# Linear attention: new order of steps (second scores ahead of values), whole tiles for the text block, copied text columns

## What is computed

```python
q = phi(x @ W_Q.T); k = phi(x @ W_K.T); v = x @ W_V.T      # phi(u) = elu(u) + 1
S = g4 * S + einsum('bhi,bhj->bhij', kt, vt)                # for each token t
z = g3 * z + kt
num = einsum('bhij,bhi->bhj', S, qt)
den = sum(z * qt, axis=-1, keepdims=True) + EPS
y = (num / den) * sigmoid(x @ W_g_w.T + W_g_b)
h = h + y @ W_O.T
h = h + quantised_ffn(layernorm(h))                         # Hadamard, 4 bits, ternary weights
```

## Time and profile before

| | us |
|---|---|
| median of 3 runs (654.33, 652.72, 647.9) | 652.72 |
| span of the profiled execution | 652.8 |
| TensorE busy, matmuls | 572.1 |
| VectorE busy | 412.4 |
| ScalarE busy | 280.9 |
| GpSimd busy | 219.3 |
| from scores(1, 1), 157.7, to scores(7, 1), 363.6 | 205.9 |

### The profile page before, as it was taken

How to read it: one execution, slowest core, us unless ns; L and a number is a source line. 1 busy time by engine, 2 the same in 40 slices (tenths; PEclk the granted TensorE clock), 3 DMA queues, 4 the chain that set the end, 5 groups by cost and what they waited for, 6 DMA issues and landing times. The chain is left out here.

```text
span 652.8 us, 11678 instructions
## 1 busy us (share of the span) xinstructions
PE 572.1 (88%) x4050; PEld 477.6 (73%) x4050; DVE 412.4 (63%) x1037; ACT 280.9 (43%) x590; POOL 219.3 (34%) x323
## 2 busy tenths in 40 slices
PE   5899859899999999899999977678887999999883
PEld 4799738677787879687868665356676899998772
DVE  2598966667778777788777775766476332222156
ACT  1533334343636455473827223474611355555310
POOL 2467760401011111111102010675003577777500
PEclk9999958899999999999999976769999999999988
DMA  7222103000000000000000060421100233333277
GB/s 231 73 62 68 40 27 97 2 1 2 1 1 2 3 0 2 2 1 1 2 2 1 3 240 2 103 68 49 49 2 24 73 101 103 106 104 101 88 226 209
DMA packets 27445, 37.03 MB, mean 57 GB/s; under 512 B 4542, under 2 KB 22783, under 8 KB 27391
## 3 DMA queue, kind: packets, MB, share of 16 engines
q1 hardware_dynamic: 23166, 24.78, 12.6%
q0 software_dynamic: 4224, 11.54, 5.7%
HBM read 25.95 MB, written 10.35 MB: 56 GB/s over the span
## 5 line engine op out<-in xcount | busy, mean ns | idle before, releaser
L1629 POOL TENSOR_TENSOR c_rstd<-c_ve,mhalf 128x2 f32<-128x2 f32 (+2 forms) x20 | 13.4, 671 | 158.3 <-DVE c_ve L564 158.3
L665 PE MATMUL ps<-b_x_hi,wa_hi 128*128 128x288 f32 x192 | 58.8, 306 | 6.0 <-DVE w1raw L1385 4.4
L2714 DVE TENSOR_TENSOR w1raw<-ps,w1raw 128x192 f32<-128x192 f32 x43 | 15.4, 358 | 68.2 <-ACT w1raw L2494 68.2
L666 PE MATMUL ps<-b_x_lo,wa_hi 128*128 128x288 f32 x192 | 57.3, 298 | 0.0
L667 PE MATMUL ps<-b_x_hi,wa_lo 128*128 128x288 f32 x192 | 57.2, 298 | 0.0
L2783 POOL DMA_INDIRECT kv<-x_rows,r_src_i x43 | 41.8, 971 | 27.1 <-issue 10.7
L1678 POOL TENSOR_TENSOR w1raw<-w1raw 128x288 f32<-128x288 f32 x16 | 16.1, 1027 | 97.8 <-DVE w1raw L1385 97.8
L1240 ACT CAST b_y_hi<-b_yt 128x256 fp32r<-128x256 f32 x32 | 12.9, 402 | 81.3 <-DVE b_yt L1367 81.2
L2307 PE MATMUL ps<-w,w1raw 96*128 x172 | 44.5, 381 | 1.3 <-ACT w1raw L2506 1.3
L665 PEld LDWEIGHTS ps<-b_x_hi,wa_hi 128*128 128x128 f32 x192 | 36.7, 191 | 9.0 <-DVE w1raw L1385 6.0
L1379 DVE TENSOR_TENSOR w1raw<-ps,decay 128x960 f32<-128x960 f32 x32 | 36.5, 1155 | 8.3 <-PE ps L1025 8.3
(11 more groups left out here) (389 smaller groups left out, 1640.5 us busy)
## 6 DMA issues: line engine op xcount, KB each, us to landing
d_x<-y_rows SPq DMA_DIRECT2D x18, 256.0 KB, 4.3
w1raw<-in_W_t SPq DMA_DIRECT2D x8, 384.0 KB, 6.0
x_rows<-w1raw SPq DMA_DIRECT2D x6, 384.0 KB, 2.5
a_xt<-in_x_t SPq DMA_DIRECT2D x8, 256.0 KB, 3.6
a_xfl<-in_x_flat SPq DMA_DIRECT2D x8, 256.0 KB, 2.8
out<-hres SPq DMA_DIRECT2D x16, 128.0 KB, 3.9
w<-in_W_t SPq DMA_DIRECT2D x8, 192.0 KB, 4.7
w1raw<-in_Ws_t SPq DMA_DIRECT2D x1, 768.0 KB, 8.7
```

Of the source, the lines that this page charges most:

```text
L665: nc.tensor.matmul(out, x_hi, w_hi, start=start, stop=False)
L666: nc.tensor.matmul(out, x_hi, w_lo, start=False, stop=False)
```

## The change

Five things, in one diff of which this is the core:

- Text block on whole tiles. Scores multiply 128 keys, so that the text keys stand in the rows where the text tile has them (`text_keys` begins 32 (b mod 4) columns ahead of the text columns of `held`; key tiles now lie ahead of query tiles there), and values use all 128 rows. The mask is zero outside the batch's own 32 rows: `move_strip` (GpSimd) writes this strip of `g["decay"]` for each batch, and `mask(b, 0)` waits for it.
- Text columns copied. Only batches 0 and 4 transpose text rows; in the others `copy_text` (GpSimd) copies 32 columns of `x_hi` and `x_lo` from the starting batch's text tile, two batches ahead.
- Other waits in `projections`: exp_done in place of phi_done, and the text values in bank 6, behind pair 2.
- Other orders: scores 2 ahead of values 0, values 2 ahead of turn_unit (TensorE); unit_sums and mask 2 ahead of take 0, quantise ahead of phi 1 (VectorE); unit_norm ahead of round_y 0 (ScalarE).
- The normalisation of rows is done a step earlier (b + 3 in place of b + 2), at the step's end.

```diff
-    return T + P if starts(b) else T
+    return T + P if starts(b) else L
+def text_copies(b):
+    return b - b // NQ
...
     for fc in range(FC):
         bank = rows_bank(b) + fc
         for t in range(2):
-            nc.tensor.transpose(ps[:, bank, t * P:(t + 1) * P], xn[:, t, fc * P:(fc + 1) * P], ident[:])
+            mm = nc.tensor.transpose(ps[:, bank, t * P:(t + 1) * P], xn[:, t, fc * P:(fc + 1) * P], ident[:])
         if starts(b):
             nc.tensor.transpose(ps[:, bank, T:T + P], xn_text[:, fc * P:(fc + 1) * P], ident[:])
-        mm = nc.tensor.transpose(ps[:, bank, L:T], xn_text[q, fc * P:(fc + 1) * P], ident[q, q])
+            mm = nc.tensor.transpose(ps[:, bank, L:T], xn_text[q, fc * P:(fc + 1) * P], ident[q, q])
...
-            first = (NP, NP + 2, 0, 2)[i]
+            first = (0, 2, NP, NP + 2)[i]
             return slice(first, first + 2)
+        def text_keys(b, j):
+            return slice(j * T + L - TXT * (b % NQ), j * T + L - TXT * (b % NQ) + P)
...
-                        mm = split_products(nc, ps[:, (6, 7, 4)[t], :], x_hi[:, b % 2, fc, rows],
+                        mm = split_products(nc, ps[:, (6, 7, 6)[t], :], x_hi[:, b % 2, fc, rows],
...
             def projections(b):
                 pe.wait_ge(lo_done, b + 1)
+                if not starts(b):
+                    pe.wait_ge(text_copied, text_copies(b))
...
-                pe.wait_ge(phi_done, NP * b + 1)
+                pe.wait_ge(exp_done, NP * b + 1)
+                pair(b, 2)
                 if starts(b):
+                    pe.wait_ge(v_read, v_count(b) + 1)
                     value_rows(b, (2,))
-                    pe.wait_ge(v_read, v_count(b + 1))
-                pair(b, 2)
-                pe.wait_ge(phi_done, NP * b + 2)
+                pe.wait_ge(exp_done, NP * b + 2)
                 pair(b, 3)
                 if b >= 2:
                     turn_q(b - 2)
-                pe.wait_ge(v_read, v_count(b) + 1)
+                pe.wait_ge(v_read, v_count(b + 1))
                 pair(b, 4)
-                pe.wait_ge(phi_done, NP * b + 3)
+                pe.wait_ge(exp_done, NP * b + 3)
...
-                    m, n = ROWS[s], WIDTHS[s]
-                    keys = slice(0, P) if s < 2 else text_rows(b)
+                    n = WIDTHS[s]
+                    keys = slice(j * T + s * P, j * T + s * P + P) if s < 2 else text_keys(b, j)
                     for r in range(2):
                         rows = slice(DK * r, DK * r + DK)
-                        mm = nc.tensor.matmul(ps[keys, bank(j) + r, col:col + n],
-                                              qk[rows, NP + j, s * P:s * P + m],
-                                              qk[rows, j, T - n:T], start=True, stop=True)
+                        mm = nc.tensor.matmul(ps[:, bank(j) + r, col:col + n], held[rows, keys],
+                                              qk[rows, NP + j, T - n:T], start=True, stop=True)
...
-                    keys = slice(0, P) if s < 2 else text_rows(b)
+                    rows = v[:, s] if s < 2 else v_text
                     for r in range(2):
                         h = 2 * j + r
                         mm = nc.tensor.matmul(ps[DK * r:DK * r + DK, 6 + j % 2, T - n:T],
-                                              v[:, s, h * DK:(h + 1) * DK] if s < 2 else
-                                              v_text[keys, h * DK:(h + 1) * DK], a[keys, j % 2, r, col:col + n],
+                                              rows[:, h * DK:(h + 1) * DK], a[:, j % 2, r, col:col + n],
...
                 if is_batch(b):
                     scores(b, 1)
+                    scores(b, 2)
                     values(b, 0)
                     values(b, 1)
-                    scores(b, 2)
                     scores(b, 3)
+                    values(b, 2)
                 if is_unit(u):
                     turn_unit(u)
                 if is_batch(b):
-                    values(b, 2)
                     values(b, 3)
...
             def round_x(b):
                 ge(act, gate_done, 2 * (b - 1))
+                if starts(b):
+                    act.wait_ge(text_copied, text_copies(b - 1))
...
-                if is_batch(b):
-                    round_y(b, 0)
                 if is_unit(u):
                     unit_norm(u)
                 if is_batch(b):
+                    round_y(b, 0)
                     round_y(b, 1)
-                if 2 <= b + 2 < B:
-                    rows_norm(nc, g, act, b + 2)
...
                     exps(n, 1)
+                    exps(n, 2)
                     if starts(n):
                         copy_v_text(n)
-                    exps(n, 2)
                     exps(n, 3)
...
+                if 2 <= b + 3 < B:
+                    rows_norm(nc, g, act, b + 3)
...
-            nc.vector.memset(ps[:, 0:2, T:], 0.0)
-            for q in range(1, NQ):
-                last = nc.vector.tensor_copy(g["decay"][TXT * q:TXT * q + TXT, :, AW - TXT:AW],
-                                             g["decay"][0:TXT, :, AW - TXT:AW])
+            step(nc.vector.memset(strips[:], 0.0))
+            for q in range(NQ):
+                nc.vector.memset(strips[text_rows(q), q:q + 1], 1.0)
+                last = nc.vector.tensor_copy(text_decay[text_rows(q), :, :], g["decay"][0:TXT, :, AW - TXT:AW])
...
             def mask(b, j):
+                if j == 0:
+                    ge(dve, strip_set, b)
...
                 if is_batch(b):
                     mask(b, 1)
-                    take(b, 0)
                 if is_unit(u):
                     unit_sums(u)
                 if is_batch(b):
+                    mask(b, 2)
+                    take(b, 0)
                     take(b, 1)
-                if 2 <= b + 2 < B:
-                    rows_sums(nc, g, dve, b + 2)
-                if is_batch(b):
-                    mask(b, 2)
                     mask(b, 3)
                     take(b, 2)
...
+                if is_unit(u):
+                    quantise(u)
                 if is_batch(n):
                     phi(n, 1)
                 if b == -1:
                     ffn_weights()
-                if is_unit(u):
-                    quantise(u)
...
+                if 2 <= b + 3 < B:
+                    rows_sums(nc, g, dve, b + 3)
                 if is_batch(n):
                     invert(n)
                     mask(n, 0)
...
+            def move_strip(b):
+                pool.wait_ge(pick_set, 4)
+                pool.wait_ge(masked, NP * b)
+                nc.gpsimd.tensor_scalar(g["decay"][:, :, AW - TXT:AW], text_decay[:],
+                                        strips[:, b % NQ:b % NQ + 1], None, ALU.mult).then_inc(strip_set, 1)
+            def copy_text(b):
+                first = T + TXT * (b % NQ)
+                pool.wait_ge(lo_done, b - b % NQ + 1)
+                ge(pool, gate_done, 2 * (b - 1))
+                nc.gpsimd.tensor_copy(x_hi[:, b % 2, :, L:T], x_hi[:, 0, :, first:first + TXT].bitcast(F32))
+                nc.gpsimd.tensor_copy(x_lo[:, b % 2, :, L:T], x_lo[:, 0, :, first:first + TXT].bitcast(F32)
+                                      ).then_inc(text_copied, 1)
...
-                if 2 <= b + 2 < B:
-                    rows_root(nc, g, pool, b + 2)
+                if 1 <= b + 2 < B and not starts(b + 2):
+                    copy_text(b + 2)
                 if is_unit(u - 1):
                     agent_root(u - 1)
+                if is_batch(b) and is_batch(n):
+                    move_strip(n)
                 if is_batch(n):
                     pool.wait_ge(phi_done, NP * n + 3)
                     for j in range(NP // 2):
                         pool.wait_ge(z_done, NP * n + j + 1)
-                        nc.gpsimd.tensor_tensor(z[:, j, :], z[:, j, :], qk[:, j, 0:T], ALU.mult).then_inc(qz_done, 1)
+                        nc.gpsimd.tensor_tensor(z[:, j, :], z[:, j, :], qk[:, NP + j, 0:T], ALU.mult
+                                                ).then_inc(qz_done, 1)
+                if 2 <= b + 3 < B:
+                    rows_root(nc, g, pool, b + 3)
```

## The result

The changed kernel takes 632.81 us in the median of 4 runs (626.41 to 634.6), the kernel before 653.33 us beside it (647.9 to 654.33): a ratio of 0.969, 95% interval 0.964 to 0.975. By these ratios the change is worth 20 and 23 us; 23.0 us were predicted. Ratios are taken over the fast runs of both kernels, medians over all runs. The profiled execution has a span of 624.7 us and is the shortest of its four, so its 28.1 us less than the profiled span before overstate the gain, and part of what follows is about which 5 to 8 us of it are not the change's.

The account below looks back on a forecast made before the run. VectorE's queue was taken to end each front, and TensorE's rear to stand at waits for phi and c_qi. The terms, the largest -11.1 us for the front, summed to -23.0 us from 652.8: 629.8 us, range 620 to 644 us.

Parts of the forecast that it names:

- Part 1: Rear, pairs 2, 3 and 5: waiting on exp_done, not phi_done, removes six stalls of 0.77 us, -4.6 us.
- part 2: Projections of a starting batch: text values in bank 6 behind pair 2 remove one wait, 0.84 us of it real, -0.8 us.
- A: Rival, text groups: whole tiles cost more than the drains they save, about 0.7 us a step, 636 us; chance 0.10.
- B: Rival: ScalarE and GpSimd are late instead, front gains only 0.6 us a step, gates hold output, 640 us; chance 0.16.
- E: Rival, front: the new order gains nothing because values 2 waits for take 0; 12.0 us go, 642 us; chance 0.09.
- D: Rival: TensorE's waits at values 2 and rotate bring the lower clock, one stretch a step, 24 us, 654 us; chance 0.05.
- C: Rival: batch 0 keeps full clock, GpSimd doesn't slow VectorE, the tail behind batch 7 shortens, 625 us; chance 0.08.
- Part 6: Scores and values: whole text tiles remove gaps and small loads, mostly hidden in fronts; exposed in scores 0, -0.5 us.
- part 5: Front, batches 1 to 7: VectorE's new queue puts rotate 8.7 us after scores 1, -11.1 us; turn_unit's waits -0.9 us.
- Parts 1 and 3: Rear: waits on exp_done save 0.77 us six times, quantise ahead of phi 1 saves 0.65 us five times, added.
- Part 7: Batch 0: front goes from 12.3 to 9 us, -3.3 us; the start of batch 0 gives -0.5 us.
- Part 4: VectorE, ahead of the reciprocal: moved rows_sums fit its idle time for two tiles; three tiles, once, cost +0.3 us.

Follow-up runs that it names:

- sums_in_front: Changed kernel with rows_sums, rows_root and rows_norm back two steps ahead, in the front, the new order of scores and values kept; 641.58 us, ratio 0.983.
- changed_again: The changed kernel itself, unedited, measured and profiled a second time against the kernel before; 630.78 us, ratio 0.965.
- the second question: Changed kernel against versions with old scores order, sums in the front, or both; fronts: old order 10.07 us without sums, 10.08 with; new order 8.51 without, 10.32 with.
- whole_tiles_old_order: Changed kernel with every move of the order undone; only whole text tiles, copied columns and GpSimd's strip stay; 653.16 us, ratio 1.004.
- strip_three_times: Changed kernel with GpSimd's strip made three times in a row for every batch; 629.69 us in one run.
- text_values_bank4: Changed kernel with a starting batch's text values back in bank 4 ahead of pair 2; 642.25 us in one run.
- round_unit_first: Changed kernel with ScalarE's c_x_hi (round_unit) ahead of round_y 2; 631.79 us, ratio 0.967; repeated, 632.26 us, ratio 0.966.
- old_front_order: Changed kernel with the old front order and rows_sums back in the front; new waits, quantise's place and whole tiles stay; 644.81 us, ratio 0.993.

## Why the prediction came out right, point by point

**What held.** The time (629.8 us against 632.8 and 630.8), the steps but for batch 2's (30.0 to 30.5 us announced for batches 1, 2, 5 and 6; 30.53, 30.80, 30.27, 30.24; the front of batch 2 is 9.04 us, since it turns the text tile of batch 4), and the front's end, 8.51 us for 8.72, right behind c_x_lo. Part 1 is 0.76 us a step for 0.77 (but see below), part 2 0.95 for 0.8. The three-tile sums cost 0.3 us (rear of batch 1 22.03 us, of batches 2 and 5 21.76), by spread_out's wait of 0.28 us. Batch 4's front lost 2.43 us, 0.6 more than the others, for the 0.9 given.

Rivals A (tiles dearer), B (ScalarE late) and E (front gains nothing) are excluded by the rows: no gap ahead of a text group, single waits of 0.4 and 0.6 us, front 1.8 us shorter. D (half clock brought by the waits of the new front, one stretch a step) fell in its size: the clock left 1.00 once between batches 1 and 6, which I had named as a sign against me, but TensorE was busy without a gap there, and it cost 1.5 us. Its mechanism is not excluded, only its place: half clock did follow a wait that the change brings, that of spread_out in the step of batch 0, in six of nine profiles, and in sums_in_front it began right behind rotate's waits of 1.1 and 1.5 us for c_x_lo in the fronts of batches 1 and 4 (162.7 and 265.1 us). Two more of my signs were touched, once each: output's loads waited 0.6 us for the gates, the loads of values 2 0.5 us (its matmuls 0.4). C (625 us) is what the profiled execution looks like, 626.41 us with batch 0 at full clock and a shorter tail; it is one execution of four, and changed_again's had neither batch 0 at full clock nor that time.

**What was mis-sized, and cancelled.**

- *Part 6, tiles: -0.5 us in all.* The statement that most of their saving lies in fronts where part 5 already sets the end is wrong as a cause. Part 5's line-up on TensorE fits only with whole tiles; on small ones the front is 9.65 us. Of the 1.80 us of a front, 1.14 go when the tiles are undone and 1.57 when the order is. The sum survived because both came together, so the right total of parts 5 and 6 owes something to luck. Its own exposed term, 0.07 us on scores 0, did not come: from scores 0 to spread_out it is 1.12 us, before 1.14, since spread_out now meets the reciprocal.
- *Parts 1 and 3: 0.77 and 0.65 us, added.* Together 1.29 us; alone the first is worth nothing, the second about 0.5 us (1.29 - 0.76). I read two waits of one stream as two terms, but with the first gone the second grows: 0.37 to 1.13 us idle ahead of turn_q.
- *Part 5's cause.* I credited the sums' removal and the new order of scores as one chain, which is right, and the square of the second question shows that the split is 0 and 0 alone, 1.57 together.
- *Part 7, batch 0: -3.3 us.* The step went from 33.21 to 29.05 us. But whole_tiles_old_order, without half clock there, has 29.66 us; so only 0.6 us of the change from it to the changed kernel is the new order (the front 1.0 us shorter, 8.77 and 7.76 us, the rear 0.4 longer, with spread_out's wait of 1.15 us in it), and most of the 4.2 us is half clock that this execution before had at 124.5 to 136.8 and this one after had not. changed_again had it and needed 32.08 us. As a term of the change it was mostly not one. The start, -0.5 us predicted and -1.3 read (scores(0, 1) at 124.48 and 123.19 us), says nothing either: with the same instructions ahead of it strip_three_times has 125.55 us.
- *Part 4, sums ahead of the reciprocal: +0.3 us.* I had read one step, that of batch 5, and given one wait for three tiles. There were three waits, 1.15 us in the step of batch 0, 0.28 in that of batch 1 and 0.26 in that of batch 4: 1.7 us. The moved sums fit only where VectorE reaches them in time, and half clock often followed the first of these waits (changed_again, above).
- *Part 8, GpSimd: +1.0 us.* Nothing. The strip takes 0.93 us (0.5 taken), the copies 0.24 each, and three strips move no step.
- *The gates: +0.7 us.* One wait of 0.6 us in seven steps, where the kernel before had one of 0.5.
- *VectorE's idle time ahead of the reciprocal near 0.* Where rows are summed, yes, as the rows of batch 1's step show. Batches 5 and 6 have none left, and 1.2 us stands there as before.

The allowances that didn't come (+0.7 and +1.0 us) and the gains that weren't the change's (most of -3.3 and -0.5 us) stand on opposite sides of the sum, beside fronts that got 0.2 us better than taken and 1.4 us of waits for the reciprocal that weren't in it. That the total came out within 3 us is in part luck; the steps of batches 1 to 6 are not.

**Where the profiled span has more.** Behind scores(7, 1) it went from 289.2 to 283.3 us, 5.9 us. 1.4 us are batch 7's front (10.58 to 9.15 us). The rest is no part of the change that I could show. The stretch from there to the end, in the kernel before, the changed one, changed_again and text_values_bank4:

```profile
363.56:652.80 289.24, 244.61 (x1415) 202.24 (x1414) 147.97 (x476) 110.79 (x284) 123.98 (x169) 0.92 0.30 93
```

```profile
341.37:624.60 283.23, 237.32 (x1415) 198.23 (x1414) 147.23 (x476) 110.58 (x284) 123.94 (x169) 0.94 0.31 95
```

```profile
344.71:627.50 282.79, 240.62 (x1415) 199.89 (x1414) 147.23 (x476) 110.60 (x284) 124.11 (x169) 0.93 0.31 95
```

```profile
349.63:640.00 290.37, 246.18 (x1415) 205.13 (x1414) 147.50 (x476) 110.62 (x284) 124.10 (x169) 0.91 0.30 93
```

text_values_bank4 runs the same instructions as the changed kernel there and takes 7 us more, at a clock of 0.91 against 0.93 and 0.94; round_unit_first has 287.6 us. So 7 us are between executions, and a span of one execution can't carry a difference of that size. The clock goes with it roughly, not strictly: 0.93 had 282.8 us.

**The sum again, with what the runs showed.** Six steps, batches 1 to 6: 205.9 us before, 189.1 after, 16.7 us less with 1.5 us of half clock in batch 3 counted against it; 18.2 us without. Batch 7's front 1.4 us. That is 19.6 us, and the start and batch 0 add what is left of them at one clock, which I can't give better than 0.6 to some 2 us. 20 to 22 us against the 20 and 23 us of the two comparisons.

## What to carry to other kernels

When two engines' queues end a stretch within a few tenths of each other, price the edits as a pair: each may be worth next to nothing alone (0.2 and 0.7 us here) and much together (1.8 us), so neither drop one because it measured as nothing nor credit one with the whole. Two waits in one stream don't add either (0 and 0.5 us alone, 1.3 us together here): move the release of the later one first. And follow one instruction's followers on the other engines before you price its move; here rows_sums cost 1.2 us on its own engine and 0.6 us through the norm behind it. Check the new place in every step, too: it was free in the step that I had read and cost 1.15 us in another.

## What the runs showed of the hardware

- Stretches of TensorE at its lower level (granted clock 0.50, 1.2 GHz), of some 3 to 7 us between 140 and 350 us, with none to four of them in a profile. TensorE was busy throughout each of them, and ahead of them it had done one of two things. Ten of 21 began right behind waits, as changed_again's at 152.2 us (1.15 us of waiting, busy 2.20 of the 3.40 us ahead). The others began where it had been busy for 0.90 to 0.99 of the 3.4 us ahead: the one at the end of batch 3 in both profiles of the changed kernel (3.40 us busy of 3.40, clock 0.51) stands in a step in which it is busy 34.3 of 34.5 us, and cost 1.5 us (34.58 against 33.08 us). Kernels with the same work on TensorE there (strip_three_times, round_unit_first) had none. Longer ones, up to 13.6 us (old_front_order, 118.4 to 132.0 us, busy 12.33 us of it), stood around the start of batch 0. What brings those without a wait is open, and the same wait had one behind it in some profiles and not in others.
- Text operands of 32 rows or columns in fp32, one group among larger ones, cost more on their own small tile than padded to a whole one, or as much: in scores 0.35 against 0.18 us where scores follow and 0.32 where values follow, in values 0.46 against 0.19 to 0.34. Two transposes of 32 rows, with the gaps around them, cost 0.6 us.
- GpSimd beside VectorE: a scalar_tensor_tensor kept its 0.76 us beside the strip, a tensor_scalar that reads one tile, and two scans went from 1.41 to 1.56 us. Beside GpSimd's products, a tensor_tensor that reads two tiles, the same phi takes 1.14 us in the kernel before and 1.12 in the changed one (at 172.42 and 203.50), as it did.
